# First-layer attention scores from rounded parts on one Trainium2 core: three products instead of one fp32 product, with GpSimd splitting keys and queries

## The chip, the cores and the metric

One core of a Trainium2 chip runs one program. The metric is the device time of that program in microseconds (us), median of three runs. The profile's span runs from the first to the last instruction of one execution. TensorE is PE in the profile, VectorE is DVE, ScalarE is ACT, GpSimd is POOL and the DMA queue's own engine is SP.

## The reference, cut to what matters

Two layers run one behind the other on 4 x 256 tokens of width 256. The first is latent attention with 16 heads and a mixture of 32 experts beside a shared one; the second is a chunked attention and a feed-forward part with low-rank experts. The change lies in the scores of the first layer:

```python
q = jnp.concatenate([q_nope, q_rope], axis=-1)
k = jnp.concatenate([k_nope, jnp.broadcast_to(k_rope, (B, S, N_HEADS, D_ROPE))], axis=-1)
scale = 1.0 / math.sqrt(D_NOPE + D_ROPE)
scores = jnp.einsum('bqhd,bkhd->bhqk', q, k) * scale
probs = jax.nn.softmax(scores, axis=-1)
attn = jnp.einsum('bhqk,bkhd->bqhd', probs, v)
```

## The kernel before, in words

Every engine has its own instruction stream, written out by hand; semaphores tie them together. `eng.wait_ge(sem, n)` holds an engine until a count is reached, and everything behind it on that engine waits too.

**Attention.** The 16 heads are worked in 8 pairs, and a pair in 8 units (one of 4 batches, one of 2 heads; 64 units in all). Keys and merged queries have 128 rows: 64 for the latent part, 64 for the rope part. A query buffer `qb[i]` holds one pair's queries, `[128, 2 heads, 1024 tokens]`; there are two, used in turn. The keys are one tile, `keys`, for all pairs. For a unit, TensorE computes `scores` (L2051), two fp32 products of 128x128 by 128x256, one for each half of the query tokens; VectorE takes the row minimum (L1575), ScalarE the exponentials (L1061), and after a normalisation TensorE turns the probabilities (`probs_turn`, L2062) three units later and multiplies them with the values (`values`, L2071) five units later, there already from rounded parts (fp32r) of the probabilities.

**The next pair's queries.** While pair p is scored, pair p+1 is prepared. TensorE merges its weights in units 0 and 1 and runs `project` (L2041) in units 2 to 5: m = 0 and 2 give the rope rows of token half c = 0 and 1, m = 1 and 3 the latent rows. The latent rows are scaled into `qb` by ScalarE (`merged_queries`, L1096, in units 4 and 6). For the rope rows VectorE multiplies by the cosines and shuffles (`rope_queries`, L1567 to L1573, at the head of units 3 and 5), and GpSimd multiplies by the sines and adds (`rotated_queries`, L843 to L853). The scratch tiles `q_plain` and `q_turned` are shared by both halves, so VectorE's second `rope_queries` waits until GpSimd's first `rotated_queries` is done (L1570), and TensorE's `project` with m = 3 waits for that second `rope_queries` (L2104).

**Experts.** Between these, TensorE works one expert in about two units: `rows_turn` (L1980) needs the expert's rows, which GpSimd gathers from memory (`gather`, L833); `gate_up` comes two places later (a unit has three places), `down` with the next expert's turn. GpSimd stores a finished expert's rows (`store`, L838). The tables of `expert_places` (L44) set the places: experts start 6 places apart, from expert 26 on 5 apart. A gather for expert e+2 is issued behind the gate of e.

**GpSimd's order in a pair before:** store and gather in unit 1, `split_rope` (L821) in unit 2, first `rotated_queries`, store and gather in unit 3, second `rotated_queries`, store and gather in unit 5, store and gather in unit 7. Ahead of each `rotated_queries` GpSimd waits until all its gathers and stores have landed (`transfers_landed`, L860).

```python
for u in range(UNITS):
    if u in (3, 5) and p + 1 < PAIRS:
        transfers_landed(gathers, stores)
        rotated_queries(p + 1, (u - 3) // 2, (p + 1) % 2)
    if u == SPLIT_AT and p + 2 < PAIRS:
        split_rope(p % 2, p // 2 + 1)
```

## Time and profile before

| | |
|---|---|
| median of 3 runs | 677.52 us (677.0 to 677.92) |
| the profiled execution, first to last instruction (its span; the page gives no other time for it) | 675.4 us |
| TensorE busy, share of the span | 654.9 us, 97% |
| VectorE, ScalarE, GpSimd busy | 500.7, 417.7, 298.5 us |
| chain that ended last | TensorE 78%, VectorE 10%, ScalarE 6% |
| first-layer scores (L2057), 256 matmul records | 66.2 us busy, 381 ns each |

Busy time counts an instruction from its start to its modelled end, so matmuls that follow each other overlap; where a text here needs what a matmul costs in a stream, it takes the distance between starts. A matmul with fp32 operands shows as two records.

### The profile page before, as it was taken

What the parts mean: (1) busy time and instruction counts of PE and PEld (TensorE: products, weight loads), DVE (VectorE), ACT (ScalarE), POOL (GpSimd) and SP (SyncE); (2) the same over time, 40 slices, a digit from 0 to 9 for tenths busy, and PEclk for the clock granted to TensorE, in tenths of its full rate; (3) what the DMA queues carried; (4) which work ended last, traced back from release to release, by engine and by line L of the source; (5) the groups of instructions that cost most, each with busy time, mean ns of one, the idle gap of its engine ahead of it and who ended that gap; (6) DMA issues with size and microseconds to landing.
All of it is one profiled execution on the core that took longest, in us unless ns stands there. A gap on an engine that the chain in (4) does not pass through costs nothing.

```text
span 675.4 us, 13827 instructions
## 1 busy us (share of the span) xinstructions
PE 654.9 (97%) x4756; PEld 573.9 (85%) x4756; DVE 500.7 (74%) x1425; ACT 417.7 (62%) x1084; POOL 298.5 (44%) x301
## 2 busy tenths in 40 slices
PE   5999999999999999999999998999999999999998
PEld 3777888898988899888888865556899999999997
DVE  6797877878778787887698788899577745645444
ACT  3766158888888888888865689998554222222221
POOL 1584146546464646452344418999532800400000
PEclk9999999999999999999999999999999999999999
DMA  8903034535535353444560000301100000000000
GB/s 316 378 5 102 1 112 128 167 116 165 165 112 191 100 180 115 123 129 125 210 257 1 1 1 1 112 1 53 75 1 1 2 17 1 1 16 1 2 16 16
DMA packets 26725, 59.43 MB, mean 88 GB/s; under 512 B 3146, under 2 KB 12748, under 8 KB 26272
## 3 DMA queue, kind: packets, MB, share of 16 engines
q1 hardware_dynamic: 23584, 50.35, 22.0%
q0 software_dynamic: 3072, 8.20, 3.7%
q8 instruction: 39, 0.64, 0.4%
q14 instruction: 30, 0.25, 0.1%
HBM read 48.24 MB, written 10.49 MB: 87 GB/s over the span
## 4 chain that ended last, share of the span: by engine, by line
PE 78%; DVE 10%; ACT 6%; issue 3%; POOL 2%; DMA 0%; ACTq 0%; POOLq 0%; DVEq 0%
PE bank L2292 10%; PE bank L2057 8%; PE bank L1991 7%; PE bank L2048 6%; PE bank L2343 5%; PE bank L2317 5%; PE bank L2077 4%; PE bank L2153 4%; PE bank L2068 4%; PE bank L1998 4%; ACT sb L1214 3%; PE bank L2119 3%; PE bank L2200 3%; PE bank L2359 3%; PE bank L1931 2%
## 5 line engine op out<-in xcount | busy, mean ns | idle before, releaser
L1073 ACT ACTIVATE sb<-bank,sb 128x256 f32<-128x256 f32 x128 | 59.6, 472 | 38.7 <-DVE sb L1578 33.5
L1281 ACT ACTIVATE h_parts<-sb 128x256 fp32r<-128x256 f32 x56 | 23.4, 418 | 76.5 <-DVE sb L1836 45.7
L2057 PE MATMUL bank<-sb 128*128 128x256 f32 x256 | 66.2, 381 | 0.0
L1578 DVE TENSOR_REDUCE sb<-bank 128x2 f32<-128x512 f32 x64 | 43.7, 683 | 27.1 <-PE bank L2057 26.6
L2292 PE MATMUL bank<-rounded,b_lo 128*128 128x256 f32 x224 | 63.0, 281 | 0.0
L2292 PE MATMUL bank<-rounded,b_hi 128*128 128x256 f32 x224 | 63.0, 281 | 0.0
L2292 PE MATMUL bank<-am_lo,b_hi 128*128 128x256 f32 x224 | 62.9, 281 | 0.0
L840 POOL DMA_INDIRECT expert_out<-sb x32 | 33.1, 1034 | 58.0 <-DVE sb L1520 44.2
L1080 ACT ACTIVATE sb<-sb 128x256 f32<-128x256 f32 x128 | 57.8, 505 | 0.1
L1827 DVE TENSOR_TENSOR sb<-sb,bank 128x256 f32<-128x256 f32 x56 | 23.4, 419 | 44.6 <-ACT sb L1238 44.5
L1238 ACT ACTIVATE sb<-bank 128x256 f32<-128x256 f32 x56 | 21.4, 382 | 53.3 <-PE bank L2292 53.3
L834 POOL DMA_INDIRECT sb<-rows_x,sb x32 | 32.8, 1026 | 42.6 <-PE bank L1991 21.2
L1991 PEld LDWEIGHTS bank<-sb 128*128 128x128 f32 (+1 forms) x384 | 46.0, 186 | 5.7 <-DVE sb L1514 3.6
L1991 PE MATMUL bank<-sb 128*128 128x128 f32 (+1 forms) x384 | 49.3, 278 | 0.8 <-DVE sb L1514 0.8
L1589 DVE TENSOR_TENSOR pt_parts<-bank,pt_parts 128x512 fp32r<-128x512 f32 x64 | 43.8, 684 | 8.5 <-ACT pt_parts L1093 6.6
L1838 DVE TENSOR_TENSOR h_parts<-sb,h_parts 128x256 fp32r<-128x256 f32 x56 | 28.7, 512 | 27.9 <-ACT h_parts L1281 27.9
L2057 PEld LDWEIGHTS bank<-sb 128*128 128x128 f32 x256 | 45.2, 190 | 4.8
L1214 ACT ACTIVATE sb<-sb 128x128 f32<-128x128 f32 (+1 forms) x128 | 46.7, 444 | 0.1
L2077 PE MATMUL bank<-pt_parts,xt_parts 128*128 128x256 f32 x256 | 46.0, 302 | 0.0
L2048 PE MATMUL bank<-rounded 128*128 128x512 f32 x160 | 42.8, 399 | 0.2 <-ACT sb L1102 0.2
L2292 PEld LDWEIGHTS bank<-rounded,b_lo 128*128 128x128 f32 x224 | 42.2, 188 | 0.0
L2292 PEld LDWEIGHTS bank<-rounded,b_hi 128*128 128x128 f32 x224 | 42.2, 188 | 0.0
(321 smaller groups left out, 1950.0 us busy)
## 6 DMA issues: line engine op xcount, KB each, us to landing
sb<-in_w_gate_up SPq DMA_DIRECT2D x32, 368.0 KB
sb<-in_w_down SPq DMA_DIRECT2D x32, 256.0 KB
sb<-in_w_pair SPq DMA_DIRECT2D x8, 704.0 KB
expert_out<-sb SPq DMA_DIRECT2D x1, 4096.0 KB, 23.5
sb<-expert_out SPq DMA_DIRECT2D x8, 512.0 KB, 6.8
sb<-in_w SPq DMA_DIRECT2D x1, 1792.0 KB, 12.9
sb<-in_b SPq DMA_DIRECT2D x1, 1792.0 KB, 7.4
sb<-in_sw_up SPq DMA_DIRECT2D x1, 1536.0 KB, 9.3
```

Of the source, the lines that this page charges most:

```text
L1073: act.activation(probs[:, u % 4, q, :], bank[3 + u % 2][:, q * S:(q + 1) * S], ACT.Exp, scale=-1.0, bias=row_min[:, u % 4, q:q + 1], accum ...
L1080: ins = act.activation(probs[:, slot, q, :], probs[:, slot, q, :], ACT.Copy, scale=row_inv[:, slot, q:q + 1])
L1214: act.activation(probs1[:, n % 4, a:b], masked[:, n % 4, a:b], ACT.Exp, scale=-1.0, bias=row_min[:, n % 4, q:q + 1]).then_inc(bl_exp, 1)
L1578: dve.tensor_reduce(row_min[:, u % 4, :], bank[3 + u % 2][:, :].rearrange("p (q n) -> p q n", q=QT), AX.X, ALU.min).then_inc(at_min, 1)
L1589: dve.tensor_tensor(r(probs_lo[:, u % 2]), bank[5 + u % 2][:, :].rearrange("p (a b) -> p a b", a=QT), probs_hi[:, u % 2], ALU.subtract).th ...
L1991: mm = pe.matmul(bank[1][0:n, to:to + P], w_gu[s][:, k, a:a + n], xeT[s][:, k, :], start=(k == 0), stop=(k == KD - 1))
L2048: mm = pe.matmul(where[:, :], r(w[i][:, cols]), r(q[:, half]), start=(n == 0), stop=(n == len(terms) - 1))
L2057: mm = pe.matmul(bank[3 + u % 2][:, q * S:(q + 1) * S], qb[i][:, h, b * S + q * P:b * S + (q + 1) * P], keys[:, h, b * S:(b + 1) * S], sta ...
L2077: mm = pe.matmul(bank[2 + 5 * h][:, 0:S], r(v_parts[:, QT * b + k, :]), r(part[:, u % 2, k, :]), start=(n == 0), stop=(n == len(terms) - 1))
L2292: mm = pe.matmul(dst, lhs, rhs, start=False, stop=(n == len(terms) - 1), skip_group_check=True)
L2317: pe.matmul(dst, r(w[:, 2 * k + j, :]), r(x[:, k, :]), start=(i + j == 0), stop=False, skip_group_check=True)
L2343: mm = pe.matmul(bank[4 + k][:, h * CW:(h + 1) * CW], r(w[:, rows_]), r(x), start=(f + h + i == 0), stop=(f == NF1 - 1 and i == 2), skip_g ...
```

## The change

Scores become six products of rounded parts for a unit, three for each token half: high queries by high keys, low queries by high keys, high queries by low keys. `keys_hi` and `keys_lo` are made once, by GpSimd, in four batches ahead of the attention. `qb_hi` and `qb_lo` are made for each pair and half by `query_halves`: two casts and two subtractions of 128x512 on GpSimd. The two query buffers become one plain `qb`. A half of it may be overwritten once its parts are made (`parts_of`), and a part once the scores that read it are done. The second `rotated_queries` moves from unit 5 to unit 6. Four semaphores are folded into others, and SP waits for the last scores before it loads the expert results.

```diff
+LAST_HALF_AT, ROTATE_AT, FIRST_HALF_AT = 1, (3, 6), 5
...
-        qb = [r2.take(2, TOK) for _ in range(2)]
+        qb = r2.take(2, TOK)
...
+            sp.wait_ge(at_s, PAIRS * UNITS)
...
+            def key_halves(b):
+                batch = slice(b * S, (b + 1) * S)
+                pool.wait_ge(latT_copied, 3 * QT * (b + 1))
+                pool.tensor_copy(r(keys_hi[:, :, batch]), keys[:, :, batch]).then_inc(key_parts, 1)
+                pool.wait_ge(key_parts, 2 * b + 1)
+                pool.tensor_tensor(r(keys_lo[:, :, batch]), keys[:, :, batch], keys_hi[:, :, batch], ALU.subtract)\
+                    .then_inc(key_parts, 1)
+            def query_halves(p, c):
+                half = slice(c * CH, (c + 1) * CH)
+                pool.wait_ge(at_qe, 6 * p + 3 * c + 3)
+                pool.wait_ge(at_qm, 2 * p + c + 1)
+                at_least(pool, at_s, UNITS * (p - 1 + c) + (UNITS // 2 if c == 0 else 0))
+                for h in range(2):
+                    pool.tensor_copy(r(qb_hi[c][:, h, :]), qb[:, h, half]).then_inc(at_parts, 1)
+                for h in range(2):
+                    pool.wait_ge(at_parts, parts_of(p, c) - 3 + h)
+                    pool.tensor_tensor(r(qb_lo[c][:, h, :]), qb[:, h, half], qb_hi[c][:, h, :], ALU.subtract)\
+                        .then_inc(at_parts, 1)
...
-                at_least(pool, at_s, UNITS * (p - 1))
+                pool.wait_ge(at_parts, parts_of(p - 1, c))
...
+            pool.wait_ge(x2_done, NT)
+            pool.wait_ge(turned, 4)
+            for b in range(2):
+                key_halves(b)
             for p in range(2):
                 split_rope(p, 0)
+                key_halves(2 + p)
+            pool.wait_ge(sh_mm, 2 * NF)
+            pool.wait_ge(latT_mm, NT)
+            query_halves(0, 0)
             pool.wait_ge(rows_out_done, 32)
-            pool.wait_ge(sh_mm, 2 * NF)
...
-                    if u in (3, 5) and p + 1 < PAIRS:
+                    if u == LAST_HALF_AT:
+                        query_halves(p, 1)
+                    if u in ROTATE_AT and p + 1 < PAIRS:
                         transfers_landed(gathers, stores)
-                        rotated_queries(p + 1, (u - 3) // 2, (p + 1) % 2)
+                        rotated_queries(p + 1, ROTATE_AT.index(u))
+                    if u == FIRST_HALF_AT and p + 1 < PAIRS:
+                        query_halves(p + 1, 0)
...
-                at_least(act, at_s, UNITS * (p - 1))
+                if p:
+                    act.wait_ge(at_parts, parts_of(p - 1, c))
...
-            def scores(g, p, u, i):
+            def scores(g, p, u):
                 b, h = u // 2, u % 2
-                pe.wait_ge(at_qe, 6 * p + 3 * (b // 2) + 3)
-                pe.wait_ge(at_qm, 2 * p + b // 2 + 1)
+                c, batch = b // 2, slice(b * S, (b + 1) * S)
+                pe.wait_ge(at_parts, parts_of(p, c))
+                if p == 0:
+                    pe.wait_ge(key_parts, 2 * b + 2)
                 at_least(pe, at_exp, 2 * g - 2)
                 for q in range(QT):
-                    mm = pe.matmul(bank[3 + u % 2][:, q * S:(q + 1) * S],
-                                   qb[i][:, h, b * S + q * P:b * S + (q + 1) * P], keys[:, h, b * S:(b + 1) * S],
-                                   start=True, stop=True)
+                    at = b % 2 * S + q * P
+                    q_hi_, q_lo_ = (w[c][:, h, at:at + P] for w in (qb_hi, qb_lo))
+                    terms = ((q_hi_, keys_hi), (q_lo_, keys_hi), (q_hi_, keys_lo))
+                    for n, (x, k) in enumerate(terms):
+                        mm = pe.matmul(bank[3 + u % 2][:, q * S:(q + 1) * S], r(x), r(k[:, h, batch]),
+                                       start=(n == 0), stop=(n == len(terms) - 1))
                 mm.then_inc(at_s, 1)
```

GpSimd's stream over a pair, in the program before, from the second rotation of one pair to the first of the next. The last words of a row name the semaphores it waits for; L840 stores, L834 gathers, L827 and L831 are `split_rope`, L848 to L852 are `rotated_queries`.

```order
L848 TENSOR_TENSOR sb<-sb 128x512 [waits y_stored1,eb_in1,at_qrope,y_stored0,eb_in0]
L851 TENSOR_TENSOR sb<-sb 64x512 [waits at_qe,at_s]
L852 TENSOR_TENSOR sb<-sb 64x512
L840 DMA expert_out<-sb 4096x256 [waits ex_y,at_qe]
L834 DMA sb<-rows_x,sb 128x256 [waits ex_g]
L840 DMA expert_out<-sb 4096x256 [waits ex_y]
L834 DMA sb<-rows_x,sb 128x256 [waits ex_g]
L840 DMA expert_out<-sb 4096x256 [waits ex_y]
L834 DMA sb<-rows_x,sb 128x256 [waits ex_g]
L827 TENSOR_TENSOR rounded<-sb 128x128 [waits pair_in1]
L827 TENSOR_TENSOR rounded<-sb 128x128
L831 TENSOR_TENSOR rounded<-sb,rounded 128x128 [waits rope_split] x2
```

The same stream in the changed program, from the halving in unit 5 on (L879 and L882 are the casts and subtractions of `query_halves`, L890 to L894 the rotation, L860 stores, L854 gathers):

```order
L879 CAST xt_parts<-sb 128x512 [waits at_s,at_qm,at_qe]
L879 CAST xt_parts<-sb 128x512
L882 TENSOR_TENSOR q_lo<-sb,xt_parts 128x512 [waits at_parts] x2
L860 DMA expert_out<-sb 4096x256 [waits ex_y]
L854 DMA sb<-rows_x,sb 128x256 [waits ex_g]
L890 TENSOR_TENSOR sb<-sb 128x512 [waits y_stored1,eb_in1,at_qrope,y_stored0,eb_in0]
L893 TENSOR_TENSOR sb<-sb 64x512 [waits at_qe,at_parts]
L894 TENSOR_TENSOR sb<-sb 64x512
L860 DMA expert_out<-sb 4096x256 [waits ex_y,at_qe]
L854 DMA sb<-rows_x,sb 128x256 [waits ex_g]
L879 CAST q_parts<-sb 128x512 [waits at_s,at_qm,at_qe]
L879 CAST q_parts<-sb 128x512
```

A halving now stands ahead of the store and gather of unit 5 and another ahead of those of unit 1, and the second rotation stands behind unit 5's gather instead of ahead of its store.

TensorE's scores of one unit in the changed program (L2116), in a unit of the first token half:

```order
L2116 MATMUL bank<-keys_hi,xt_parts 128x256 [waits at_exp,key_parts,at_parts]
L2116 MATMUL bank<-keys_hi,q_lo 128x256
L2116 MATMUL bank<-keys_lo,xt_parts 128x256
L2116 MATMUL bank<-keys_hi,xt_parts 128x256
L2116 MATMUL bank<-keys_hi,q_lo 128x256
L2116 MATMUL bank<-keys_lo,xt_parts 128x256
```

Six products stand where two fp32 products (L2057) stood; nothing else moved on TensorE.

## Rows read from the trace of the kernel before

**Rows 1.** Steady attention, 105 to 320 us: busy PE, PEld, DVE, ACT, POOL; clock, DMA, GB/s

```profile
105.00:320.00 215.00, 213.46 (x1403) 191.50 (x1402) 169.28 (x444) 178.41 (x504) 114.08 (x117) 1.00 0.45 140
```

**Rows 2.** Waits of TensorE, 105 to 320 us, longest: us in total, times, longest

```profile
PE bank L1983 <- DVE sb L1528: 1.2, 2, 0.9
```

**Rows 3.** Timeline of TensorE, pair 5: start us, us, engine line op

```profile
237.67 1.03 PE L2057 MATMUL bank<-sb 128*128 128x256 f32 x4
...
256.75 1.03 PE L2057 MATMUL bank<-sb 128*128 128x256 f32 x4
257.61 0.38 PE L1983 MATMUL bank<-sb 128*128 128x128 f32 x2
...
259.61 0.39 PE L2048 MATMUL bank<-rounded 128*128 128x512 f32 x1
...
268.27 1.03 PE L2057 MATMUL bank<-sb 128*128 128x256 f32 x4
```

**Rows 4.** Chain that ended last: twelve rounded products on end, second layer

```profile
657.81 1.43 PE bank L2292 x12
```

**Rows 5.** Timeline of GpSimd, pair 5; in brackets the idle time before, and its releaser

```profile
251.23 1.09 POOL L848 TENSOR_TENSOR sb<-sb 128x512 f32<-128x512 f32 x1
...
253.81 1.26 POOL L852 TENSOR_TENSOR sb<-sb 64x512 f32<-64x512 f32 x1
255.87 1.05 POOL L840 DMA_INDIRECT expert_out<-sb  x1 [0.80 <-POOL sb L852]
257.23 1.02 POOL L834 DMA_INDIRECT sb<-rows_x,sb  x1 [0.30 <-issue]
260.26 1.09 POOL L848 TENSOR_TENSOR sb<-sb 128x512 f32<-128x512 f32 x1 [2.01 <-issue]
```

**Rows 6.** Timeline of GpSimd, second layer: two casts and two subtractions of 128x512

```profile
458.18 1.17 POOL L946 CAST rounded<-sb 128x512 fp32r<-128x512 f32 x2
459.31 2.53 POOL L949 TENSOR_TENSOR am_lo<-sb,rounded 128x512 fp32r<-128x512 f32 x2
```

**Rows 7.** Timeline of VectorE, pair 5, second `rope_queries`

```profile
257.50 0.67 DVE L1571 TENSOR_TENSOR sb<-bank,sb 128x512 f32<-128x512 f32 x1
...
258.11 0.72 DVE L1573 STREAM_SHUFFLE sb<-bank 128x512 f32<-128x512 f32 x1
```

**Rows 8.** Timeline of GpSimd: a split behind a gather, and the first rotation

```profile
94.86 1.00 POOL L834 DMA_INDIRECT sb<-rows_x,sb  x1 [6.14 <-PE bank L1991]
95.88 0.78 POOL L827 TENSOR_TENSOR rounded<-sb 128x128 fp32r<-128x128 f32 x2
...
98.25 1.10 POOL L848 TENSOR_TENSOR sb<-sb 128x512 f32<-128x512 f32 x1 [0.77 <-DVE sb L1573]
```

**Rows 9.** Timeline of TensorE, last pair: rows of experts 29 and 30

```profile
306.78 0.44 PE L1983 MATMUL bank<-sb 128*128 128x128 f32 x2
...
313.18 0.44 PE L1983 MATMUL bank<-sb 128*128 128x128 f32 x2 [0.88 <-DVE sb L1528]
```

**Rows 10.** Timeline of VectorE ahead of the attention: last rope rows of the first half

```profile
81.93 0.68 DVE L1632 TENSOR_TENSOR sb<-sb 64x512 f32<-64x512 f32 x1
```

**Rows 11.** Timelines ahead of the attention: GpSimd's first gather; TensorE's first scores

```profile
86.12 1.23 POOL L834 DMA_INDIRECT sb<-rows_x,sb  x1 [14.96 <-DVE sb L1511]
...
88.53 1.03 PE L2057 MATMUL bank<-sb 128*128 128x256 f32 x4
```

**Rows 12.** Timeline of VectorE, before the attention: one instruction beside a busy GpSimd, one not

```profile
68.13 1.47 DVE L1494 TENSOR_TENSOR sb<-sb 128x1024 bf16<-128x1024 f32 x1
...
71.28 1.22 DVE L1494 TENSOR_TENSOR sb<-sb 128x1024 bf16<-128x1024 f32 x1
```

**Rows 13.** Timeline of GpSimd, second layer: the casts and subtractions at their slowest

```profile
535.67 1.56 POOL L946 CAST rounded<-sb 128x512 fp32r<-128x512 f32 x2
537.20 2.72 POOL L949 TENSOR_TENSOR am_lo<-sb,rounded 128x512 fp32r<-128x512 f32 x2
```

**Rows 14.** All rotations' first instruction on GpSimd: ns min/median/max, first and last start

```profile
L848 POOL TENSOR_TENSOR sb<-sb x14: 1091/1092/1101, 98.2 to 290.4; 128x512 f32<-128x512 f32 x14
```

More of the change, by code:

```diff
@@ L332, in program @@
             end = 0
+            keys_hi = over("keys_hi", start[0], 2 * TOK)
+            q_parts1 = over("q_parts1", start[0] + 2 * NT * D, 2 * 2 * CH)
+            q_lo0 = over("q_lo0", start[1] + 2 * TOK, 2 * CH)
+            keys_lo = over("keys_lo", start[3] + KEYS_AT, 2 * TOK)
+        with ExitStack() as overlay:
+            end = 0
             su_lo = over("su_lo", start[1] + SU_AT, KD * 2 * NF * P)
@@ L438, in program @@
         r2 = strip(region2)
-        qb = [r2.take(2, TOK) for _ in range(2)]
+        qb = r2.take(2, TOK)
+        by_half = [w.rearrange("p (h n) -> p h n", h=2) for w in
+                   (xt_parts[:, 0:2 * CH], q_parts1[:, 0:2 * CH], q_lo0[:, :], q_parts1[:, 2 * CH:4 * CH])]
+        qb_hi, qb_lo = by_half[0:2], by_half[2:4]
+        keys_hi, keys_lo = (w[:, :].rearrange("p (h n) -> p h n", h=2) for w in (keys_hi, keys_lo))
         r2.at = SU_AT
@@ L574, in program @@
         cf_in, rows_in, proj_in = (sem(n) for n in ("cf_in", "rows_in", "proj_in"))
-        shared_in, zero_set = (sem(n) for n in ("shared_in", "zero_set"))
+        shared_in, pool_first = (sem(n) for n in ("shared_in", "pool_first"))
         ln_stats, ln_mv, ln_var, ln_sd, ln_rstd = (sem(n) for n in ("ln_stats", "ln_mv", "ln_var", "ln_sd", "ln_rstd"))
@@ L614, in program @@
         b13_split, am_split = sem("b13_split"), sem("am_split")
-        fill_mm, fill_out, step_mask, low_rank = (sem(n) for n in ("fill_mm", "fill_out", "step_mask", "low_rank"))
+        fill_mm, fill_out, low_rank = (sem(n) for n in ("fill_mm", "fill_out", "low_rank"))
         bl_q, bl_bias, bl_s, bl_min, bl_exp, bl_inv, bl_t, bl_even, bl_odd, bl_v, bl_oT, bl_turn, bl_o = (
@@ L626, in r, with parts_of @@
             return ap.bitcast(F32R)
+        def parts_of(p, c):
+            return 8 * p + 4 * c + 4
         def merged(w):
@@ L1094, in copy_probsT, with merged_queries @@
                                ACT.Copy).then_inc(at_tout, 1)
-            def merged_queries(p, c, i, where):
+            def merged_queries(p, c, where):
                 half = slice(c * CH, (c + 1) * CH)
                 act.wait_ge(at_q, 4 * p + 2 * c + 2)
-                at_least(act, at_s, UNITS * (p - 1))
-                act.activation(qb[i][0:KVL, 0, half], where[0:KVL, :], ACT.Copy, scale=Q_SCALE)
-                act.activation(qb[i][KVL:P, 1, half], where[KVL:P, :], ACT.Copy, scale=Q_SCALE).then_inc(at_qm, 1)
+                if p:
+                    act.wait_ge(at_parts, parts_of(p - 1, c))
+                act.activation(qb[0:KVL, 0, half], where[0:KVL, :], ACT.Copy, scale=Q_SCALE)
+                act.activation(qb[KVL:P, 1, half], where[KVL:P, :], ACT.Copy, scale=Q_SCALE).then_inc(at_qm, 1)
             for c in range(2):
-                merged_queries(0, c, 0, bank[5])
+                merged_queries(0, c, bank[5])
             for p in range(PAIRS):
@@ L1630, in first_queries @@
                 dve.wait_ge(at_qe, 3 * c + 1)
-                dve.tensor_tensor(qb[0][DR:P, 0, half], q_plain[DR:P], q_turned[DR:P], ALU.add).then_inc(at_qe, 1)
-                dve.tensor_tensor(qb[0][0:DR, 1, half], q_plain[0:DR], q_turned[0:DR], ALU.add).then_inc(at_qe, 1)
+                dve.tensor_tensor(qb[DR:P, 0, half], q_plain[DR:P], q_turned[DR:P], ALU.add).then_inc(at_qe, 1)
+                dve.tensor_tensor(qb[0:DR, 1, half], q_plain[0:DR], q_turned[0:DR], ALU.add).then_inc(at_qe, 1)
             for i in range(NT):
@@ L2084, in pair @@
                     g = UNITS * p + u
-                    scores(g, p, u, i)
+                    scores(g, p, u)
                     experts(p, u, 0)
```

34 lines of the change are left out of this document (18 added, 16 removed).

## The prediction

> **What bounds the kernel now.** I read the windows first. Through the steady attention TensorE is busy 213.5 of 215 us at a granted clock of 1.00, while VectorE (169 us), ScalarE (178) and GpSimd (114) have room [rows 1]. The list of TensorE's waits agrees: the longest entry is 1.2 us in two waits [rows 2]. So TensorE's work sets the pace. Its timeline gives that pace: pair 5 lasts from 237.67 to 268.27, which is 30.60 us [rows 3]. GpSimd is idle half of the time, but its timeline shows what fills a pair there: transfers with gaps around them, rotations, and about 2 us from the end of a gather to the rotation that waits for its landing [rows 5]. That stream is what the change lengthens, so busy shares are not enough; I add it up as a loop.
>
> **The change, part by part.**
>
> *Scores on TensorE.* A unit's two fp32 products take from 256.75 to 257.61, 0.86 us from start to start [rows 3]. Twelve rounded products of the same shape, each with weights of its own, take 1.43 us on end [rows 4], 0.119 us each; six take 0.71. A unit saves 0.15 us, a pair 1.2, all 64 units 9.6. With TensorE as the bound a pair would then last 29.4 us.
>
> *Halving the queries on GpSimd.* Two casts and two subtractions of 128x512 run from 458.18 to 461.84 (459.31 + 2.53): 3.66 us [rows 6]. Their ends in the new attention: 3.66 at best and, with the slow rows of the second layer, 535.67 to 539.92, 4.25 us [rows 13]. I take 3.66, because the rotations' instructions on GpSimd in the attention never vary (1091 to 1101 ns in all 14) [rows 14]. [...]
>
> *A transfer behind a halving.* A store now follows a subtraction it doesn't wait for; no row shows this, so I bound the gap g. A tensor instruction behind a gather starts 0.02 us after it (95.86 to 95.88) [rows 8]: the lower end. A store behind a rotation whose end it awaits starts after 0.80 us: the upper end. A gather queued behind a store starts after 0.30 us [rows 5]. That last is nearest, since nothing is awaited there either. Tensor instructions on end even overlap by some 0.04 us (two casts of 0.61 in 1.17) [rows 6], so a tensor ahead in place of a transfer should make the gap a little shorter: g = 0.24.
>
> *GpSimd's loop over a pair*, which the order shows as two like halves:
> - rotation, store, gather: 251.23 to 258.25 (257.23 + 1.02), 7.02 us [rows 5]
> - halving: 3.66
> - gap g: 0.24
> - store, gather: 255.87 to 258.25, 2.38 us
> - landing until the next rotation: 258.25 to 260.26, 2.01 us [rows 5]. In unit 3 `split_rope` stands between; half of it takes 0.78 [rows 8], so some 1.6 fit inside the landing.
>
> That is 15.31 a half, 30.62 us a pair, or 30.14 + 2g. TensorE's pair is 29.4. **GpSimd becomes the bound.** It is loaded for 30.62 us where TensorE took 30.60 before, so six steady pairs come out level and the gain on TensorE turns into waiting. Nothing makes GpSimd itself wait: what it needs from the others (the gate of unit 3, the latent rows of unit 4, the store rows of unit 5) is ready by more than 1 us.
>
> *Where TensorE is caught.* VectorE's second `rope_queries` waits for the end of the first rotation, 3.84 us after its start (253.81 + 1.26 less 251.23); then come its 1.33 us [rows 7], then `project` with m = 3. Before, the latter began 8.4 us behind the rotation's start (259.61 less 251.23) [rows 3, 5], so there are some 3 us of slack. Behind the waiting VectorE instruction is the row minimum of unit 5, behind that ScalarE's exponentials, needed by TensorE three units later. Scores have room: parts of half 0 are done 10.7 us behind the rotation's start, the next pair's first scores come some 15 us behind it.
>
> *The chain to the end.* The first rotation started at 98.25 behind VectorE [rows 8]; cheaper scores bring it to 97.9. The seventh, six loops later, starts at 281.6. In the last pair the experts stand closer. The rows of expert 29 are gathered behind the second rotation of pair 6, where before that gather only waited for a gate: 281.6 + 15.31 + 7.02 + 2.01 = 305.9 when they have landed. TensorE took them at 306.78 before [rows 9], so it is 0.9 us ahead there, after a wait of about 3 us. Behind that point expert steps set the pace (TensorE idles 0.88 us at 313.18 for expert 30 already [rows 9]), and of the five saved scores I count 0.4.
>
> *Ahead of the attention.* Four key halvings of a cast and a subtraction each, some 1.9 us, 7.5 in all, fill a GpSimd that idled 14.96 us before its first gather [rows 11]. They can slow VectorE: 1.47 us against 1.22 beside a busy GpSimd [rows 12]. Bounds are 0 and some 0.5 us on TensorE; I take 0.1. The first query halving can start when VectorE's rope rows are done at 82.61 [rows 10] and ends at 86.3, ahead of the first scores at 88.53 [rows 11]. The first gather slips from 86.12 to about 86.6 [rows 11]; its rows are used behind the scores of the second unit, so I give it no cost. That the second buffer goes costs nothing: a half of `qb` is overwritten units after its parts exist. SP's new wait for the last scores costs nothing, since the last expert's `down` stands behind those scores on TensorE. The folded semaphores cost nothing: those instructions run in the same order.
>
> **Sum**, against the profiled execution: -0.9 - 0.4 + 0.1 = -1.2 us, a span of 674.2. The median of the runs lies 2.1 above the span of 675.4, so the forecast is 677.5 - 1.2 = **676.3 us**. Because g enters thirteen times, the change of time is -4.3 + 13g. A measurement of this kernel tells about 0.2% (1.35 us) from no change.
>
> **The rivals.**
> - *The transfer's start is hidden by the subtraction.* g = 0.02: loop 30.18 us, -4.0 us, 673.5. For it: the instructions on GpSimd overlap at their ends [rows 6]. Against: 0.30 behind a transfer [rows 5].
> - *TensorE stays the bound.* Were the loop shorter than 29.4 us, the whole 9.6 less some 0.6 in the last pair would come: 668.5. Against: it needs more than 1.2 us out of a loop in which each piece is a row.
> - *A transfer pays its full start behind any tensor instruction.* g = 0.80: loop 31.74 us, +6.1 us, **slower**, 683.6. The place is the store of units 1 and 5; the change gets slower from g = 0.33 on. For it: each store behind a rotation shows 0.80 [rows 5]. Against: there the end is awaited.
> - *Halvings meet VectorE.* 4.25 instead of 3.66 us, thirteen times, +7.7: 684.0. For it: rows 13. Against: rows 14.
> - *It doesn't do what it says:* the rounded products could cost no less than fp32 in place, through loads of weights that don't hide. Then TensorE's pair stays at 30.6, level with GpSimd's loop, and the time is 678 to 680. Against: rows 4 has a new load for each product.
>
> **How the numbers follow.** Forecast (loop 30.4 to 30.9) 0.47; start hidden 0.22; TensorE bound 0.08; full start 0.11; contention 0.07; not as said, or a late start of the attention, 0.05. The range takes in the forecast's case, the hidden start and the slow end up to g = 0.75, and leaves out the bare TensorE bound and the far end of the two slow cases, some 0.2 in all: 672.0 to 683.0. Faster by over 0.2%: TensorE bound, nearly all of the hidden start and a third of the forecast's case, 0.43. Slower: the two slow cases, a quarter of the forecast's own and part of the last, 0.29. The rest, 0.28, is no change.
>
> **What would show it.** Right: scores six records to a unit with 0.71 us from first start to the next instruction; GpSimd near 85 to 90% busy between 105 and 300 us, its rotations 30.6 us apart from pair to pair; GpSimd's wait before a rotation is only the 2 us of landing; VectorE's L1571 in unit 5 waits for GpSimd; TensorE idle about 1.2 us a pair at `project`, and 3 us once in unit 2 of the last pair. Wrong: rotations less than 29.6 apart or TensorE without idle time (TensorE is the bound), GpSimd's subtractions above 1.4 us (contention), or a store 0.8 us behind a subtraction.

## The result, and the profile after

The changed kernel takes 683.67 us (680.72 to 685.95, 6 runs) against 677.35 (676.78 to 677.92, 6 runs) for the kernel before on the same chip: ratio 1.0092, 95% interval 1.0073 to 1.0111. It is slower by 6.3 us where 1.2 us less was forecast, and it lies outside the range. The profiled execution took 683.9 us, its span is 682.0.

The steady attention, as in [rows 1], and the longest of TensorE's waits, here from 85 to 345 us where [rows 2] has 105 to 320 (us in total, times, longest):

```profile
105.00:320.00 215.00, 206.82 (x1481) 188.82 (x1479) 167.40 (x439) 175.26 (x500) 167.11 (x174) 0.99 0.45 140
```

```profile
PE bank L2044 <- DVE sb L1567: 3.4, 8, 0.7
PE bank L2036 <- DMA sb<-rows_x,sb: 3.2, 2, 2.8
PE bank L2036 <- DVE sb L1581: 1.2, 2, 0.9
PE bank L2090 <- DVE rounded L1609: 0.7, 1, 0.7
```

The chain that ended last, shares by engine, has gone from 78% TensorE to this:

```profile
PE 45%; POOL 16%; issue 13%; DVE 13%; DMA 6%; ACT 6%; POOLq 0%; ACTq 0%; DVEq 0%
```

From 105 to 320 us TensorE lost 6.6 us of busy time and GpSimd gained 53. GpSimd is still busy for only 152.7 of the 195 us from 105 to 300 (78%), where the prediction gave 85 to 90% as a sign of being right. The new entry at the top is L2044, an expert's `gate_up` that waits for VectorE's copy of the rows; no step of the prediction speaks of it.

GpSimd from one first rotation (257.02) to the second (272.42), as in [rows 5]:

```profile
257.02 1.09 POOL L890 TENSOR_TENSOR sb<-sb 128x512 f32<-128x512 f32 x1 [0.75 <-DMA sb<-rows_x,sb]
258.25 1.29 POOL L893 TENSOR_TENSOR sb<-sb 64x512 f32<-64x512 f32 x1
259.62 1.27 POOL L894 TENSOR_TENSOR sb<-sb 64x512 f32<-64x512 f32 x1
261.69 1.04 POOL L860 DMA_INDIRECT expert_out<-sb  x1 [0.80 <-POOL sb L894]
263.04 1.02 POOL L854 DMA_INDIRECT sb<-rows_x,sb  x1 [0.30 <-issue]
264.07 1.17 POOL L879 CAST xt_parts<-sb 128x512 fp32r<-128x512 f32 x2
265.20 2.52 POOL L882 TENSOR_TENSOR q_lo<-sb,xt_parts 128x512 fp32r<-128x512 f32 x2
267.89 1.04 POOL L860 DMA_INDIRECT expert_out<-sb  x1 [0.17 <-issue]
269.24 1.02 POOL L854 DMA_INDIRECT sb<-rows_x,sb  x1 [0.31 <-issue]
272.42 1.09 POOL L890 TENSOR_TENSOR sb<-sb 128x512 f32<-128x512 f32 x1 [2.16 <-DMA sb<-rows_x,sb]
```

A halving takes 3.65 us (265.20 + 2.52 less 264.07), and the store behind it starts 0.17 us after its end: both disputed prices came out as taken, or a little better. From the second rotation on, all that the rotations wait for is landings. Still, from the first rotation (101.80) to the thirteenth (287.75) six loops take 185.95 us, 31.0 each, where the prediction had 30.62.

The beginning of the attention moved too. The first rotation started at 98.25 before [rows 8], was forecast for 97.9 and started at 101.80. Two stretches of the same timeline with GpSimd and VectorE together show a part of it:

```profile
60.74 1.26 POOL L869 TENSOR_TENSOR keys_lo<-sb,keys_hi 128x512 fp32r<-128x512 f32 x1
60.83 1.20 DVE L1535 TENSOR_SCALAR sb<-sb 128x32 f32<-128x32 f32 x1
...
63.18 0.33 PE L2012 MATMUL bank<-sb 128*128 128x128 f32 x1 [1.52 <-DVE rounded L1520]
...
86.37 2.55 POOL L882 TENSOR_TENSOR q_lo<-sb,xt_parts 128x512 fp32r<-128x512 f32 x2
86.43 1.26 DVE L1555 TENSOR_SCALAR sb<-sb 128x32 f32<-128x32 f32 x1
...
87.81 1.16 DVE L1558 SCALAR_TENSOR_TENSOR sb<-sb 128x32 f32<-128x32 f32 x1
```

In the kernel before, the first of these VectorE instructions is one row:

```profile
60.23 0.18 DVE L1482 TENSOR_SCALAR sb<-sb 128x32 f32<-128x32 f32 x1
```

It took 0.18 us there; beside a subtraction of GpSimd it took 1.20 and ended when that ended (60.83 + 1.20 = 62.03 against 60.74 + 1.26 = 62.00).

Last, TensorE at the rows of expert 29 in the last pair, and its granted clock around them (the windows' columns here are length, busy PE, clock, DMA share, GB/s):

```profile
312.29 0.41 PE L2036 MATMUL bank<-sb 128*128 128x128 f32 x2 [2.83 <-DMA sb<-rows_x,sb]
```

```profile
310.00:312.00 2.00, 0.00 (x0) 1.00 0.47 168
312.00:314.00 2.00, 1.71 (x11) 0.90 0.18 63
314.00:316.00 2.00, 2.00 (x12) 0.50 0.50 134
316.00:318.00 2.00, 2.00 (x15) 0.75 0.24 67
318.00:320.00 2.00, 1.11 (x11) 1.00 0.78 226
```

The forecast had this wait at about 3 us, and it is 2.83. What it didn't have: from some 1 us behind its end the granted clock is 0.50 for some 3 us.

### The profile page after: what moved, and what is told of

Same layout as the page of the kernel before. It is cut to its first block, busy times and chain, and to the rows that moved or that the text cites. A ratio compares the mean times of both kernels' runs of the same rounds, so it can differ in the third digit from the quotient of the medians.

```text
span 682.0 us, 14177 instructions
## 1 busy us (share of the span) xinstructions
PE 652.4 (96%) x4884; PEld 575.7 (84%) x4884; DVE 505.1 (74%) x1425; ACT 416.5 (61%) x1084; POOL 366.6 (54%) x373
## 4 chain that ended last, share of the span: by engine, by line
PE 45%; POOL 16%; issue 13%; DVE 13%; DMA 6%; ACT 6%; POOLq 0%; ACTq 0%; DVEq 0%
PE bank L2350 10%; DMA sb<-rows_x,sb 6%; PE bank L2401 5%; PE bank L2375 5%; PE bank L2211 4%; ACT sb L1267 3%; PE bank L2258 3%; POOL expert_out L860 3%; PE bank L2417 2%; POOL sb L894 2%; PE bank L2177 2%; POOL sb L890 2%; PE bank L1984 2%; POOL sb L854 2%; PE bank L2286 2%
## 5 line engine op out<-in xcount | busy, mean ns | idle before, releaser
L2044 PEld LDWEIGHTS bank<-sb 128*128 128x128 f32 (+1 forms) x384 | 46.9, 190 | 10.1 <-DVE sb L1567 9.0
L2044 PE MATMUL bank<-sb 128*128 128x128 f32 (+1 forms) x384 | 50.6, 283 | 3.9 <-DVE sb L1567 3.4
L860 POOL DMA_INDIRECT expert_out<-sb x32 | 33.2, 1037 | 26.8 <-DVE sb L1573 12.7
L2350 PEld LDWEIGHTS bank<-rounded,b_lo 128*128 128x128 f32 x224 | 42.2, 189 | 0.0
L2350 PEld LDWEIGHTS bank<-rounded,b_hi 128*128 128x128 f32 x224 | 42.2, 188 | 0.0
L2350 PEld LDWEIGHTS bank<-am_lo,b_hi 128*128 128x128 f32 x224 | 42.1, 188 | 0.0
L1849 DVE CUSTOM_DVE_ANT_1 sb<-bank,sb 128x128 f32<-128x128 f32 (+1 forms) x128 | 37.9, 353 | 5.1 <-PE bank L2309 5.1
L854 POOL DMA_INDIRECT sb<-rows_x,sb x32 | 32.9, 1029 | 12.1 <-issue 9.0
```

The costliest lines, as they stand in the source:

```text
L854: pool.indirect_dma_start(xe[:, s, :], None, rows_x2[:, :], bass.IndirectOffsetOnAxis(ap=source[:, e:e + 1], axis=0), bounds_check=TOK - 1 ...
L860: pool.indirect_dma_start(res[:, :], bass.IndirectOffsetOnAxis(ap=dest[:, e:e + 1], axis=0), ye[:, s, :], None, bounds_check=TOK * TOPK0 - ...
L1849: dve.tensor_tensor_reduce(masked[:, n % 4, a:b].rearrange("p (n c) -> p n c", c=CHUNK), bank[SCORE_BANK[n % 4]][:, a:b].rearrange("p (n c ...
L2044: mm = pe.matmul(bank[1][0:n, to:to + P], w_gu[s][:, k, a:a + n], xeT[s][:, k, :], start=(k == 0), stop=(k == KD - 1))
L2350: mm = pe.matmul(dst, lhs, rhs, start=False, stop=(n == len(terms) - 1), skip_group_check=True)
```

## The experiments

"The changed kernel" is the one above; its line numbers shift by one to three in some of the runs.

**Is GpSimd's loop the bound?** `hi_only` takes work from TensorE alone, `no_halves` from GpSimd alone.

```diff
# hi_only
-                    terms = ((q_hi_, keys_hi), (q_lo_, keys_hi), (q_hi_, keys_lo))
+                    terms = ((q_hi_, keys_hi),)
# no_halves
-            return 8 * p + 4 * c + 4
+            return 4 * c + 4
...
-                    if u == LAST_HALF_AT:
+                    if u == LAST_HALF_AT and not p:
...
-                    if u == FIRST_HALF_AT and p + 1 < PAIRS:
-                        query_halves(p + 1, 0)
```

> The two products with low parts are left out of the scores (two matmuls a unit in place of six); every halving on GpSimd stays. Theory (GpSimd's loop is the bound of the steady attention): a pair still takes 30.8 to 31.1 us from rotation to rotation, the time is 681 to 683.5, and the 0.47 us a unit taken from TensorE turns into idle time there. Rival (TensorE or its clock is the bound, or most of the +6 comes from its side): 64 x 0.47 = 30 us go, time about 654.

> The halvings of pairs 1 to 7 are left out (their scores use pair 0's parts); scores, rotations and transfers stay. GpSimd's loop falls by 7.4 us to some 23.5, so TensorE sets the pace, and its pair can be read. Theory of the prediction (29.4 us a pair): time 672 to 674 with the late start of the changed kernel. Rival (the rounded scores uncover small waits at L2044 for VectorE's copy, 0.26 to 0.45 us each, that the longer fp32 scores hid): a pair of 30.0 to 30.2 us, time 676 to 678.

`hi_only`: 685.24 us (683.72 to 686.69), ratio 1.0104 (1.0076 to 1.0132). Two thirds of the scores' products go and nothing comes back; from 105 to 300 us TensorE is busy 172.7 of 195 us. The rival's 654 us is out. The theory's figures were a little low all the same: its six loops take 31.4 us each, not 30.8 to 31.1, and the time lies 1.7 us above its range; the landings, 3.3 to 4.2 us from a gather to the second rotation, are longer than in the changed kernel, and why is open. `no_halves`: 676.34 us (675.51 to 676.89), ratio 0.999 (0.998 to 1.000). So GpSimd's halvings in the loop cost 6 to 7 us. But even without them the gain on the kernel before, 676.91 us beside it, is only 0.6 us. The late start (below) is still in that time; TensorE's timeline shows the other reason. Two rows, one pair apart:

```profile
207.04 1.60 PE L2042 MATMUL bank<-sb 128*128 128x128 f32 x12 [0.26 <-DVE sb L1565]
...
237.24 1.60 PE L2042 MATMUL bank<-sb 128*128 128x128 f32 x12 [0.26 <-DVE sb L1565]
```

A pair takes 30.20 us, not 29.4. Set side by side with the kernel before, TensorE gains 0.15 us at each of the eight scores, as forecast (1.2 a pair), and gives back 0.27 at the `gate_up` of unit 1, 0.25 at the projection of unit 4 and 0.31 at the `gate_up` of unit 7: 0.83. These are waits that the longer fp32 scores had just covered. In the kernel before VectorE's copy ends 0.05 us ahead of the `gate_up` of unit 7 that needs it:

```profile
144.03 0.41 DVE L1514 COPY sb<-bank 128x256 f32<-128x256 f32 x1
...
144.49 1.59 PE L1991 MATMUL bank<-sb 128*128 128x128 f32 x12
```

**Can the order of VectorE give the 0.31 back?**

```diff
# no_halves_copy
-                    if u == HIDDEN_FIRST:
+                    if u in (HIDDEN_FIRST, 7):
                         experts(p, u, 0)
                     minimum(g, u)
...
-                    if u != HIDDEN_FIRST:
+                    if u not in (HIDDEN_FIRST, 7):
                         experts(p, u, 0)
```

> As no_halves, and in unit 7 VectorE copies the expert's rows ahead of the row minimum in place of behind it. If the order of VectorE's two instructions is what L2044 waits for, the wait of 0.26 to 0.45 us there goes, a pair gets 0.2 to 0.45 us shorter, and the time falls by 1.5 to 3 against no_halves. Rival (the wait moves to the row minimum's users, or is of another cause): within 0.7 of no_halves.

677.68 us (676.38 to 678.17), ratio 1.0011 (1.0001 to 1.0021): 1.3 us more than `no_halves`. The wait at `gate_up` is gone and one of 0.15 us for the experts' hidden values (L2034) has come in each pair, which still takes 30.20; in the last pair TensorE now waits 0.95 and 0.42 us for the low parts of the probabilities. The rival's mechanism held, the wait moved to another user; its time, within 0.7 us of `no_halves`, did not. Neither this order nor the one of `best_merge` below shortens the pair.

**What delays the start?** Three kernels hold GpSimd's subtractions back from VectorE's routing.

```diff
# keys_late, and both_late
             pool.wait_ge(turned, 4)
+            pool.wait_ge(rt_dest, 1)
             for b in range(2):
                 key_halves(b)
# subs_late, and both_late
+                if p + c == 0:
+                    pool.wait_ge(rt_dest, 3)
                 for h in range(2):
                     pool.wait_ge(at_parts, parts_of(p, c) - 3 + h)
```

> GpSimd starts its first key halving only when VectorE's first routing sum is done (one wait added), so that no subtraction of it runs beside VectorE's L1535 and L1537. Theory (a small VectorE instruction is held until a running GpSimd subtraction ends, and that delays TensorE at L2012): L1535 takes 0.18 us again instead of 1.20, TensorE's wait at L2012 falls from 1.52 to 0.1 or 0.2, the attention starts 1.2 to 1.5 us earlier, time 1.2 to 1.8 below the changed kernel's 683.7. Rival (no holding; L1535's length has another cause, or the delay is absorbed later): L1535 stays near 1.2, or the time stays within 0.5 of 683.7.

> The two subtractions of the very first query halving wait until VectorE's routing is through (its third sum), so they no longer run beside L1555 and L1558. Theory (holding): L1555 and L1558 take 0.18 us each instead of 1.26 and 1.16, the first gather starts about 2 us earlier, but the first low parts of the queries come later; the time falls by 0.5 to 1.5. Rival (the first gather's start is not what delays the attention, the halving itself is): no gain, or 0.5 to 1 slower.

> Both waits together: key halvings after VectorE's first routing sum, the first query halving's subtractions after its last. Theory (a small VectorE instruction waits for a running GpSimd subtraction, and the two places are separate costs): L1535, L1555 and L1558 take about 0.18 us each, the first rotation starts some 2.5 to 3 us earlier than in the changed kernel (101.8), 39 to 40 us behind the routing sum instead of 42.2; time 679 to 680.5. Rival (one place hides the other, or GpSimd's own later start eats it): no better than the runs with one wait, 681.5.

`keys_late`: 681.46 us (677.63 to 682.56), ratio 1.004 (1.002 to 1.006). `subs_late`: 681.51 (678.14 to 685.87), 1.0055 (1.0031 to 1.0078). `both_late`: 680.59 (676.06 to 683.44), 1.0056 (1.0034 to 1.0078). Each wait cures its own instruction and leaves the other; the first row is of `keys_late`, the second of `subs_late`:

```profile
59.40 0.18 DVE L1536 TENSOR_SCALAR sb<-sb 128x32 f32<-128x32 f32 x1
```

```profile
85.57 0.18 DVE L1557 TENSOR_SCALAR sb<-sb 128x32 f32<-128x32 f32 x1
```

The first 60 us differ by up to 1.6 us from one profile to another, so the start is read from VectorE's routing sum (the 128x1024 reduction at 57.97 to 59.58) to the first rotation: 39.3 us before, 42.2 in the changed kernel, 40.8 with `keys_late`, 41.1 with `subs_late`, 39.8 with both. The start costs 2.9 us, and the two places make up 2.4 of it. The subtractions that `subs_late` and `both_late` hold back meet another instruction of VectorE's, an addition of 64x512 that takes 0.69 us alone; here it is in `subs_late`:

```profile
88.69 1.64 DVE L1686 TENSOR_TENSOR sb<-sb 64x512 f32<-64x512 f32 x1
```

The rows show what each wait cures: L1535 at 1.20 us in the changed kernel and 0.18 in `keys_late`, L1555 at 1.26 and 0.18 in `subs_late`. The medians of the three kernels don't show a gain in time: their intervals overlap that of the changed kernel run again (`after_again` below, 1.0051 to 1.0096), since these kernels spread by 5 to 8 us from run to run, the kernel before by 2 to 3. `best` against `rot_cover`, further below, shows the gain in time.

**What makes the loop 31 us?** The profile of `both_late`, of the shortest of its runs (span 674.3), has loops of 30.11 to 30.14 us in its last three. Its GpSimd and DMA queue ahead of a second rotation:

```profile
231.87 0.33 SPq L746 DMA_DIRECT2D sb<-in_w_gate_up  x1
232.03 1.04 POOL L860 DMA_INDIRECT expert_out<-sb  x1 [0.17 <-PE bank L2047]
233.38 1.01 POOL L854 DMA_INDIRECT sb<-rows_x,sb  x1 [0.31 <-issue]
235.28 0.33 SPq L750 DMA_DIRECT2D sb<-in_w_down  x1
236.33 1.09 POOL L892 TENSOR_TENSOR sb<-sb 128x512 f32<-128x512 f32 x1 [1.94 <-DMA sb<-rows_x,sb]
```

And the same place of the changed kernel:

```profile
268.73 0.33 SPq L750 DMA_DIRECT2D sb<-in_w_down  x1
269.24 1.02 POOL L854 DMA_INDIRECT sb<-rows_x,sb  x1 [0.31 <-issue]
271.84 0.33 SPq L746 DMA_DIRECT2D sb<-in_w_gate_up  x1
272.42 1.09 POOL L890 TENSOR_TENSOR sb<-sb 128x512 f32<-128x512 f32 x1 [2.16 <-DMA sb<-rows_x,sb]
```

Over the profiles of the changed kernel (two), `keys_late`, `subs_late` and `both_late`, a second rotation starts 2.93 us behind the start of the gather (median of 15) where the load of `w_down` is issued 1.5 to 2.2 us behind the gather, and 3.27 us (median of 16) where it is issued up to 0.7 us ahead of it. In the first group `w_gate_up` was issued 1.3 to 1.8 us ahead of the gather, so no landing here is free of loads. The groups overlap: 3.40 and 3.57 us stand in the first, 2.98 and 4.92 in the second. The other four of the 35 landings, with `w_down` 0.65 to 1.3 us behind the gather, took 3.35 to 4.25. TensorE triggers the loads, GpSimd's position decides the gathers; the theory is that once GpSimd falls behind by some 2 us, each landing meets a load. The next kernels test this; `after_again` is the changed kernel unaltered.

```diff
# down_behind, both_down (with both_late), before_down (in the kernel before)
                 sp.wait_ge(ex_done, e + 1)
+                sp.wait_ge(eb_in[s], 16 * ((e + SETS) // SETS + 1))
                 expert_down(e + SETS, s)
# no_down
                 sp.wait_ge(ex_done, e + 1)
-                expert_down(e + SETS, s)
...
-                pe.wait_ge(ed_in[s], 16 * before + 16)
+                pe.wait_ge(ed_in[s], 16)
```

> SP starts an expert's w_down load only when the same expert's rows have landed (one wait added in SP's queue). Seen so far: GpSimd's landing wait ahead of the second rotation is 2.1 to 2.4 us where the w_down load is issued 0.5 us ahead of the gather (the changed kernel), and 1.83 to 1.94 where it is issued 2 us behind it (the profile of both_late, whose loop takes 30.11). Theory (the two collide, and that keeps GpSimd's loop at 31.0 instead of 30.1): landing waits fall to 1.8 to 1.95, a loop to 30.1 to 30.3, time 677.5 to 679.5, and the runs spread less. Rival (the landing depends on something else): landing waits stay above 2.1, time 682.5 or more.

> both_late and down_behind together. Theory (start of the attention 2.7 us, collisions 4 to 5 us, both independent): every run near the fast profile of both_late, 675 to 677, a little under the kernel before. Rival (something else makes the slow runs of both_late): 679 to 681 with a spread of 5 us or more.

> The changed kernel unaltered, on the same chip as the three beside it, as their measure: 683 to 684.5, with a spread of some 4 us between runs; in its profile, loops of 30.1 us where w_down is issued behind the gather and 30.7 to 31.3 where it is issued ahead of it.

> The kernel before, with the same added wait of SP. Theory (there TensorE's own chain sets the pace and a landing has slack): no change, within 0.7 us of the kernel before. Rival (the collisions cost the kernel before as well, or the later load is missed): more than 1 us off.

> The changed kernel without the w_down loads of experts 2 to 31 (they use the first two experts' weights). Theory (a landing takes longer because loads are in flight): gather to rotation 2.8 to 2.9 us at the second rotations (3.1 to 3.4 in the changed kernel), loops 30.1 to 30.4, time 678 to 680. Rival (the landing is long for another reason, or w_gate_up and the pair's weights alone do it): gather to rotation still 3.1 or more, time 682 or more.

`down_behind`: 686.34 us (684.72 to 688.05), ratio 1.0136 (1.0117 to 1.0156). `both_down`: 684.22 (683.07 to 685.45), 1.0101 (1.0085 to 1.0117). Both forecasts fell. From the timelines, us from the start of a gather to that of the rotation behind it, pairs 2 to 6:

```
                     second rotations               first rotations
changed kernel       3.22 3.13 3.44 3.18 3.37       3.25 3.02 3.12 3.39 3.09
both_late            3.03 2.92 2.95 2.87 2.92       3.64 2.93 2.80 2.78 2.84
down_behind          3.01 2.99 3.41 2.89 2.86       3.78 4.68 4.79 4.64 2.82
no_down              3.29 2.92 3.17 2.86 2.87       2.84 2.94 3.46 3.15 2.84
```

The second rotations got their short landings, as the theory said. But in SP's stream the pair's weights (four loads, 704 KB and more) and `w_gate_up` stand behind the `w_down` that now waits, and they moved into the gather ahead of the first rotation. There GpSimd waits, in `down_behind`, first for the rope weights and then for the rows:

```profile
222.46 1.02 POOL L855 DMA_INDIRECT sb<-rows_x,sb  x1 [0.31 <-issue]
225.25 0.78 POOL L848 TENSOR_TENSOR rounded<-sb 128x128 fp32r<-128x128 f32 x2 [1.77 <-DMA sb<-in_w_rope]
225.99 0.88 POOL L852 TENSOR_TENSOR rounded<-sb,rounded 128x128 fp32r<-128x128 f32 x2
227.25 1.09 POOL L891 TENSOR_TENSOR sb<-sb 128x512 f32<-128x512 f32 x1 [0.39 <-DMA sb<-rows_x,sb]
```

In the last loop, where no pair's weights are left to load, `down_behind` runs at 30.2 us and `both_down` at 30.1. `after_again`: 682.57 us (679.95 to 685.59), ratio 1.0073 (1.0051 to 1.0096), its loops 30.9 to 31.7, none of 30.1 as expected, not even the first, where the second landing, with `w_down` behind the gather, took 2.94. `before_down`: 677.82 (676.89 to 678.51), 1.0005 (0.9996 to 1.0013): in the kernel before, landings have slack. `no_down`: 682.25 (680.92 to 683.83), 1.0076 (1.0061 to 1.0090). Its profile has six loops in 183.1 us, 30.5 each, nearer to the theory's 30.1 to 30.4 than to 31.0, but the time is as in the rival: the same end as in the changed kernel follows, 2.95 us of waiting for expert 29 and a clock of 0.50 from 308 to 314 us. So landings with loads in flight were longer: by 0.3 us in the medians (3.27 against 2.93) where `w_down` went just ahead of the gather, and by 1.2 to 1.7 where several were moved into it (4.64 to 4.79 against 3.02 to 3.39). But two second rotations of `no_down` are long (3.29, 3.17) without any `w_down`; that `w_down` alone holds the loop at 31 is not shown.

**Two ways to take GpSimd out of the bound that missed.** `rot5` covers one landing with a halving, `subs_dve` gives VectorE two of the four subtractions a pair.

```diff
# rot5
-LAST_HALF_AT, ROTATE_AT, FIRST_HALF_AT = 1, (3, 6), 5
+LAST_HALF_AT, ROTATE_AT, FIRST_HALF_AT = 1, (3, 5), 5
...
+                    if u == FIRST_HALF_AT and p + 1 < PAIRS:
+                        query_halves(p + 1, 0)
                     if u in ROTATE_AT and p + 1 < PAIRS:
                         transfers_landed(gathers, stores)
# subs_dve
-                for h in range(2):
+                for h in range(0 if c else 2):
...
+            def last_half_low(p):
+                dve.wait_ge(at_parts, 8 * p + 6)
+                for h in range(2):
+                    dve.tensor_tensor(r(qb_lo[1][:, h, :]), qb[:, h, CH:2 * CH], qb_hi[1][:, h, :], ALU.subtract)\
+                        .then_inc(at_parts, 1)
...
+                    if u == LOW_AT:
+                        last_half_low(p)
```

> The second rotation moves from unit 6 to unit 5, and the first halving of the next pair goes ahead of it, so that this halving covers one of the two landings (2 us) that GpSimd stands idle for. Theory (GpSimd's loop of 31.0 us sets the pace): the loop falls to about 28.9, below TensorE's 29.4; TensorE is the bound, a pair takes 29.4 to 29.8 us, seven pairs give back 8 to 11 us: 673 to 676, below the kernel before too. Rival (the landings are not what is paid; TensorE cannot go faster because of its own waits or contention): a pair stays at 30.6 or more, time 681 to 684.

> The two subtractions of each pair's last half move from GpSimd to VectorE (unit 2). GpSimd's loop falls by 2.5 to about 28.5 us, below TensorE's pair. Theory (GpSimd's loop is the bound, TensorE's own floor is 30.1): a pair takes 30.0 to 30.3 us, time 678 to 679.5. Rival (VectorE's added 1.4 us a pair, or subtractions held by GpSimd, makes VectorE's chain the limit): pair 30.8 or more, time 683 or more.

`rot5`: 681.53 us (680.04 to 683.76), ratio 1.0062 (1.0042 to 1.0082); loops 29.9 to 31.2. A gather now has a halving, a rotation and a store between it and the next, 10.7 us (260.38 to 271.09), and at `rows_turn` TensorE waits four times for rows, 4.8 us in all, and twice, 1.6 us, with no releaser in the profile. `subs_dve`: 682.89 (682.23 to 683.62), 1.0082 (1.0065 to 1.0099); GpSimd is relieved, yet a pair takes 31.1 us evenly: TensorE's projections of units 3 and 4 lose 0.34 and 0.44 us against the kernel before, behind VectorE and ScalarE. With the 0.27 and 0.31 at the `gate_up`s that `no_halves` shows too, 1.36 us are lost, more than the 1.2 saved; the last 0.3 or so of the 31.1 is spread over smaller gaps. The rival of its forecast held. Both kernels also run against the floor of 30.2 that `no_halves` shows.

**Covering the landing.** GpSimd waited for the landings ahead of a whole rotation. Now the multiplication and the addition to the lower partitions go first.

```diff
# rot_cover, best, best_merge; before_cover in the kernel before
                 pool.tensor_tensor(turned_q, turned_q, along(table("q_sin"), (1, CH // S)), ALU.mult).then_inc(at_qe, 1)
...
-                pool.tensor_tensor(qb[DR:P, 0, half], q_plain[DR:P], q_turned[DR:P], ALU.add).then_inc(at_qe, 1)
                 pool.tensor_tensor(qb[0:DR, 1, half], q_plain[0:DR], q_turned[0:DR], ALU.add).then_inc(at_qe, 1)
+                transfers_landed(*landed)
+                pool.tensor_tensor(qb[DR:P, 0, half], q_plain[DR:P], q_turned[DR:P], ALU.add).then_inc(at_qe, 1)
...
-                        transfers_landed(gathers, stores)
-                        rotated_queries(p + 1, ROTATE_AT.index(u))
+                        rotated_queries(p + 1, ROTATE_AT.index(u), (gathers, stores))
# best: also the two waits of both_late. best_merge: also, in ScalarE's unit()
+                if p + 1 < PAIRS and u == 4:
+                    merged_queries(p + 1, 0, bank[0])
                 if not (isinstance(g, int) and g < CONTEXT_LAG):
```

> In each rotation GpSimd does the multiplication (128 partitions) and the addition to the lower partitions first, and waits for the transfers' landing only ahead of the last addition. Some 2.4 us of its own work then cover the landing; nothing else changes. Theory (GpSimd's loop with its landings is the bound behind the start; TensorE's floor is 30.2 as in no_halves): the loop could run in 28.5, so pairs follow TensorE at 30.2 to 30.3; the changed kernel's 6 loops take 181 to 182 us in place of 186 to 187, time 676.5 to 678.5, and the runs spread by less than 2 us. Rival (the landings are not what separates 31 from 30.2): 682 or more.

> rot_cover with the two added waits of both_late. Theory (start and loop are the two costs of the change, and add up): 2.5 to 3 us below rot_cover, 674 to 675.5, below the kernel before (677.4) by 0.3 to 0.5%. Rival (the two overlap): within 1 us of rot_cover.

> As best, and in unit 4 ScalarE copies the merged queries first, ahead of its two copies for other units. TensorE's projection there started 0.25 us late in every pair of no_halves for lack of that copy. Theory: 0.2 us less a pair, 1 to 1.5 us less than best. Rival (the delayed copies make TensorE wait elsewhere): same as best or up to 2 us more.

> The kernel before, with its rotations in the order of rot_cover. Theory (there GpSimd's loop had room, so its landings cost nothing, and what best gains on the kernel before is the change's own): within 0.7 us of the kernel before, 677.4. Rival (the cover itself is worth something without the change): 675.5 or less.

| kernel | median us (range) | ratio to before | 95% interval |
|---|---|---|---|
| rot_cover | 676.20 (675.62 to 677.06) | 0.9986 | 0.9977 to 0.9995 |
| best | 674.31 (673.68 to 674.74) | 0.9952 | 0.9939 to 0.9965 |
| best_merge | 674.00 (673.82 to 675.08) | 0.9955 | 0.9942 to 0.9968 |
| before_cover | 677.38 (676.21 to 677.92), before beside it 678.09 | 0.9987 | 0.9978 to 0.9996 |

One edit of order takes 6 to 7 us off the changed kernel (682.57 and 683.67, on other chips) and its spread from 5 us to 1.4. GpSimd in `rot_cover`, a second and then a first rotation:

```profile
262.71 1.03 POOL L854 DMA_INDIRECT sb<-rows_x,sb  x1 [0.30 <-issue]
263.77 1.10 POOL L890 TENSOR_TENSOR sb<-sb 128x512 f32<-128x512 f32 x1
265.01 1.27 POOL L893 TENSOR_TENSOR sb<-sb 64x512 f32<-64x512 f32 x1
266.53 1.27 POOL L895 TENSOR_TENSOR sb<-sb 64x512 f32<-64x512 f32 x1 [0.26 <-DMA sb<-rows_x,sb]
...
280.68 1.08 POOL L890 TENSOR_TENSOR sb<-sb 128x512 f32<-128x512 f32 x1 [3.06 <-DVE sb L1626]
```

The landing costs 0.26 us where the rows of the changed kernel had 2.16, and at the next rotation GpSimd waits 3.06 us for VectorE: it has room again. Six loops take 180.93 us, 30.2 each, which is TensorE's floor of `no_halves`; the wait for expert 29 is gone and the clock stays at 1.00. `best` adds the earlier start: 39.7 us from routing sum to first rotation, and 1.9 us less than `rot_cover`, with intervals that don't meet. The start and the loop add up. It beats the kernel before by 3.1 us, of which some 0.7 to 0.9 could be had without the change (`before_cover`, at the edge of what can be told). `best_merge` gives nothing that can be told from `best`: the 0.25 us at the projection turned up at unit 7's `gate_up`, whose wait grew from 0.26 to 0.45.

No kernel without `transfers_landed` was tried, so what a landing costs altogether stays an inference from the waits.

## Why the prediction was wrong

The forecast's span was 674.2, the profiled span 682.0. By its own steps:

- *GpSimd becomes the bound*: right, shown by `hi_only` and `no_halves`. Halving 3.66 (3.64 to 3.69 seen in the loops), g = 0.24 (0.17 seen); the rivals g = 0.80 and slow halvings beside VectorE fell at the first row. The step from rows 14, that GpSimd isn't slowed in the attention, was right.
- *Landing until the next rotation, 2.01 us*: **mis-sized.** The value was one row; seen were 1.9 to 2.6 us at the second rotations and 0.4 to 1.2 left over behind `split_rope` at the first, where the prediction's 2.01 less 1.6 leaves 0.4. From gather to rotation that makes 2.9 us too much in six loops; the cheaper g gave 0.8 back. The loop came to 31.0 instead of 30.62, 2.2 us over six loops. The step took a DMA's landing for a constant although it now stood in the bound, and did not ask what else the DMA queues carry at that moment.
- *Ahead of the attention, 0.1 us*: **the step that failed most.** Seen were 2.9 us. It compared long VectorE instructions beside GpSimd (1.47 against 1.22) and set 0 to 0.5; what is hit are VectorE's small instructions on the routing chain, of which three (L1535, L1555, L1558) lost 1.0 to 1.1 us each, and the chain feeds TensorE at L2012 and the first gather. "The first gather slips from 86.12 to about 86.6" became 90.54. Of the profile's 3.9 us against 97.9, another 0.6 lie ahead of 59 us, where executions vary, and 0.35 were the scores' expected gain.
- *Contention was read from one side.* For the halvings the prediction weighed it by whether GpSimd gets slower (1091 to 1101 ns in rows 14). Beside a subtraction of GpSimd's that took 1.26 us, VectorE's L1535 took 1.20 us instead of 0.18; they ended at 62.00 and 62.03 us.
- *TensorE's pair is 29.4*: **wrong, 30.2**, and hidden by the bound. Eight times 0.15 us was right; 0.83 of the 1.2 goes back into three waits for VectorE and ScalarE that fp32 scores had covered. The rival "TensorE stays the bound", 668.5, did not come even where GpSimd had room: `no_halves` gives 676.34, `best` 674.31.
- *TensorE is caught at expert 29, after a wait of about 3 us*: right in place and size (2.83), as was what it hangs on (24.5 us behind the thirteenth rotation, 24.3 forecast). *Of the five saved scores I count 0.4*: instead TensorE needed 1.1 us more than before from there to the last scores, with the lower clock in that stretch.

Sum against the forecast: 3.9 at the first rotation, 2.2 in six loops, 0.2 to expert 29, and 1.5 behind it, 7.8 us. The wrong 29.4 adds nothing to it, since the slower loop stood over it: it was luck that this error had no effect.

## What to carry to other kernels

An engine whose list of waits is nearly empty can still be tied to others to within 0.05 us: before crediting a saving on it, look up for each later instruction when its inputs were ready, since the first that was just in time takes the saving. Where a change turns a queue into the bound, every landing in it counts in full (GpSimd waited 1.9 to 2.6 us at the second rotations) and may vary with what else is in flight (medians of 2.93 and 3.27 us from gather to rotation, by when `w_down` was issued), so look for work of the same engine that may run during the landing. And new work in an engine's idle time is not free when another engine's instructions are held up beside it, as 0.18 us became 1.16 to 1.26 here: look which short instructions of that engine lie on a chain there.

## What the runs showed of the hardware that was not expected

- Three VectorE instructions of 128x32 from SBUF to SBUF (0.18 us alone) took 1.16 to 1.26 us beside a GpSimd subtraction of 128x512, and ended with it (62.03 us against 62.00, 88.97 against 88.92). The GpSimd side stretched too: the subtraction that started at 70.10, 0.11 us behind a VectorE instruction with two SBUF inputs, took 2.23 us instead of 1.26, and a subtraction of VectorE's that started in it took 1.12 instead of 0.69. VectorE's reads of PSUM (L1519, 0.28 to 0.29 us) and its reciprocal (L1637, 0.15 to 0.16 us) did not stretch beside such a subtraction.
- A store behind a halving's subtraction, which is not awaited, started 0.17 us after it (265.20 + 2.52 to 267.89), behind the awaited addition of a rotation 0.80 (259.62 + 1.27 to 261.69).
- From the start of a gather of 128 rows to the rotation that waits for it: mostly 2.9 to 3.1 us with `w_down` issued 1.5 us or more behind it, 3.1 to 3.5 with it just ahead, and up to 4.8 with several loads. Why is not shown.
- The length of a stall does not settle what the clock does behind it. At waits of 2.83 and 2.90 us for expert 29's rows (the two profiles of the changed kernel), 2.95 (`keys_late`, `no_down`), 4.03 (`hi_only`), and also 2.28 (`down_behind`) and 2.17 (`both_down`), the granted clock was 0.50 for 3 to 7 us. At 2.81 in `subs_late` and 1.88 in `rot5` it stayed at 1.00. From expert 29's rows to the last scores it took 17.4 us in the kernel before, and 18.5 to 19.8 in the two profiles of the changed kernel and in `no_down`: 1.1 to 2.4 us beyond the stall's own length.
- In `both_late` the drop goes with the longer runs. Of its ten, five have a mean clock of 1.000 and took 676.1 to 680.3 us, five have 0.997 and took 680.9 to 683.4. `after_again` has a run of 685.28 us with a mean clock of 1.000. That the clock alone makes the difference is not shown: the same late GpSimd that makes TensorE stall has cost time before.
